# One transformer layer on one core: inverse norms of q and k by eight VectorE steps in place of two GpSimd powers

## The chip, the cores and the metric

The kernel runs on one core of a Trainium2 chip. The metric is the device time of one execution, in microseconds (us); of several executions the median is taken. A core has five engines with a queue each, which run in order and wait for one another by semaphores: TensorE (PE), VectorE (DVE), ScalarE (ACT), GpSimd (POOL) and SyncE (SP, which here only issues DMAs).

## The reference

The input is 32 images of 3x96x96 pixels, cut into 36 patches each: 1152 rows of 768 numbers. The layer is, shortened:

```python
h = layernorm(patches) @ W + b          # 768 -> 192
h = layernorm(h, g2, b2)
x = _layernorm(h); q, k, v = split(x @ in_proj.T + bias)
attn = einsum('nhld,nhmd->nhlm', _normalize(q), _normalize(k))   # 12 heads of 16
attn = softmax(attn * exp(min(logit_scale, ...)))
h = h + (attn @ v * head_scale) @ out_w.T + out_b
y = bitlinear(_layernorm(h), w_in, g_in)         # rms norm, 8-bit rows, ternary weights
up, gate = split(y)
h = h + bitlinear(silu(gate) * up, w_out, g_out)
```

`_normalize` divides each head's 16 numbers of q and of k by their length: a row has 24 inverse square roots of sums of squares. Attention runs over the 32 images at one patch place.

## The kernel before, in words

The 1152 rows are nine tiles of 128 rows, t = 0 to 8, four patch places each. Every tile passes the same stages, and every engine has one list, written out by hand, that interleaves the stages of different tiles. A step is a small function named after what it writes (`ss_(3)` writes `ss` of tile 3), and waits for semaphores that count tiles. Nothing but these lists and waits sets the order.

The stages of a tile, with the engine:

- Embedding: `bst1_`, `mv1_` (DVE: statistics of the pixels), `xp_` (ACT), `xT_` (PE: transposes into banks 0 and 1), `xTe` (ACT), `emb` (PE, bank 7), `ve1_` and `rs1_` (POOL: variance plus epsilon, then power -0.5), `h0s_` (DVE).
- Second norm: `bst2_`, `mv2_`, `hg_`, `h_` (DVE) with `ve2_`, `rs2_` (POOL). Third norm: `bst3_`, `mv3_` (DVE), `ve3_`, `rs3_`, `nm3_` (POOL), `xh_` (ACT).
- q, k, v: `xhT_`, `qkv` (PE), `sq_` (ACT: squares), `qkc`, `vx_` (ACT: copies), `ss_` (DVE: sums of squares, 24 a row), `ssm_` (DVE: these with the logit scale). Then `rnk_` (L317) and `rnq_` (L313), two POOL powers of 12 numbers a row each, and the products `kpad_` (L818) and `qn_` (L809) on DVE, which scale k and q. `kT_` (L828) and `qT_` (L824) are DVE's transposes of them.
- Attention: `sc` (PE, L613: scores), `mx_`, `sm_` (DVE), `pr_` (ACT: exp), `pT_` (DVE, L841), `pv` (PE, L625), `rsum_`, `on_` (DVE), `oT_` (PE, bank 1), `oTe` (ACT), `proj` (PE), `h2_` (DVE, L854).
- First feed-forward product: `bst4_`, `mv4_`, `xc_`, `ax4_` (DVE), `ve4_`, `s4_` (POOL), `an4_`, `ri4_`, `qs4_` (DVE, L878 to L886: the scale of the 8-bit row), `xq_` (ACT), `xqT_` (PE, L648, bank 3), `xqTe` (ACT), `ff1` (PE, L658, banks 2 and 3), `f_h_`, `c5_` (POOL), `th_` (ACT), `yg_`, `yy_` (DVE, L890 and L895: they read banks 2 and 3).
- Second: `yw_` (POOL, L343, 512 wide), `ysq_` (ACT), `ms5_`, `r5_`, `s5_` (POOL), `ax5_`, `an5_`, `ri5_`, `qs5_` (DVE), `yq_` (ACT), `yqT_` (PE), `yqTe` (ACT), `ff2` (PE), `f2_` (POOL), `out_` (DVE, L917), and two DMAs that store the tile.

Weights are prepared in the first third, between the tiles' steps.

Of the kernel before, what the change touches and what calls it, by code (L numbers as in the profile page):

```python
# [42 lines left out]
def vit_layer(nc, x, ln1_g, ln1_b, w_emb, b_emb, ln2_g, ln2_b, w_in_proj, b_in_proj, logit_scale,  # L43
              head_scale, w_out_proj, b_out_proj, w_ff_in, g_in, w_ff_out, g_out, out):
    ctx = ExitStack()
    with ctx:
# [216 lines left out]
        def _(pool):  # L263
# [17 lines left out]
            def ve1_(t):  # L281
                pool.wait_ge(mv1_ok, t + 1)
                nc.gpsimd.tensor_scalar(ve1[:, t, :], mv1[:, t, 1:2], LN_EPS, None, ALU.add).then_inc(ve1_ok, 1)  # L283

# [689 lines left out]
```

## Time and profile before

| what | value |
|---|---|
| median of 3 runs | 154.35 us (154.21 to 155.75) |
| the profiled execution's own time | 155.63 us |
| its span, first to last instruction | 153.8 us |
| PE busy | 109.4 us, 71% |
| VectorE busy | 109.2 us, 71% |
| ScalarE busy | 83.7 us, 54% |
| GpSimd busy | 103.8 us, 68% |
| mean granted TensorE clock | 0.897 of full speed |

The profile is of one execution. A busy time is the part of the span in which an engine works. A group of instructions is shown with its summed time and the mean of one; a wait is the idle time of an engine ahead of an instruction, with what ended it.

### The profile page before, as it was taken

Reading aid. Unit: us, or ns where it says so; the run is one execution under the profiler, and the core shown is the slowest. Engines: PE = TensorE matmul, PEld = TensorE weight load, DVE = VectorE, ACT = ScalarE, POOL = GpSimd, SP = SyncE. Lnnn points to the kernel's source line nnn. Section 1 sums busy time; section 2 is a strip of 40 time slices with the busy share of each in tenths; the row PEclk is TensorE's granted clock in tenths of the full one; section 3 lists DMA queues with packets and bytes.
Section 4 is the critical chain, followed back from the end, with each engine's and each line's share of the span. In section 5 each row is a group of like instructions: output and inputs, shape, how many; then the busy total and the mean of one; then the engine's idle time right before and its main releaser. Section 6 shows DMA issues by size and latency. Waiting matters only on the chain.

```text
span 153.8 us, 4558 instructions
## 1 busy us (share of the span) xinstructions
PE 109.4 (71%) x1784; PEld 84.5 (55%) x1784; DVE 109.2 (71%) x342; ACT 83.7 (54%) x168; POOL 103.8 (68%) x178
## 2 busy tenths in 40 slices
PE   0008997878897889749999879789855966762540
PEld 0008995666786578637878646646634744330320
DVE  3066059849899688846898988976999988747310
ACT  0318435999769273444385667345755366685610
POOL 5006026769599999996589899897988636835500
PEclk9999999999999999975899999758999699689555
DMA  5999999930000000000000000100000000000000
GB/s 105 227 281 185 167 267 203 182 101 2 2 4 0 4 4 0 0 4 4 2 0 4 0 4 4 29 15 11 5 27 4 4 26 15 17 12 27 12 25 26
DMA packets 24092, 7.74 MB, mean 50 GB/s; under 512 B 20038, under 2 KB 23495, under 8 KB 24072
## 3 DMA queue, kind: packets, MB, share of 16 engines
q1 hardware_dynamic: 20310, 6.43, 20.8%
q10 hardware_dynamic: 3762, 1.03, 3.5%
q8 instruction: 14, 0.23, 0.7%
q14 instruction: 6, 0.05, 0.1%
HBM read 6.58 MB, written 0.88 MB: 49 GB/s over the span
## 4 chain that ended last, share of the span: by engine, by line
POOL 34%; PE 28%; DVE 13%; issue 8%; ACT 8%; DMA 4%; ACTq 2%; DVEq 0%; POOLq 0%
POOL rn L317 10%; POOL rn L313 9%; PE bank L658 4%; DMA xs<-in_x_dram 4%; PE bank L583 3%; PE bank L666 3%; DVE bst L751 3%; PE bank L675 3%; PE bank L613 3%; POOL rs L297 3%; PE bank L625 3%; PE bank L518 2%; ACT yq L492 2%; POOL rs L289 2%; ACTq L226 2%
## 5 line engine op out<-in xcount | busy, mean ns | idle before, releaser
L317 POOL TENSOR_TENSOR rn<-ssm,mhalf 128x12 f32<-128x12 f32 x9 | 20.5, 2281 | 2.8 <-DVE ssm L803 2.5
L313 POOL TENSOR_TENSOR rn<-ssm,mhalf 128x12 f32<-128x12 f32 x9 | 21.3, 2372 | 0.4
L583 PE MATMUL bank<-w_emb_g,xT 128*128 128x192 f32 x108 | 20.7, 345 | 1.0 <-DVE h0s L762 1.0
L583 PEld LDWEIGHTS bank<-w_emb_g,xT 128*128 128x128 f32 x108 | 18.7, 202 | 1.5 <-issue 1.5
L574 PE MATMUL bank<-ident,xp 128*128 128x128 f32 x54 | 8.1, 290 | 13.7 <-ACT xp L431 12.2
L343 POOL TENSOR_TENSOR yw<-yy,gout_bc 128x512 f32<-128x512 f32 x9 | 11.4, 1267 | 8.3 <-DVE yy L895 8.2
L574 PEld LDWEIGHTS bank<-ident,xp 128*128 128x128 f32 x54 | 6.7, 149 | 14.1 <-issue 12.9
L751 DVE BATCH_NORM_STATS2 bst<-xs 128x6 f32<-128x384 f32 x18 | 8.7, 540 | 6.6 <-DMA xs<-in_x_dram 6.6
L601 PE MATMUL bank<-w_qkv,xhT 97*128 97x384 f32 (+1 forms) x36 | 12.9, 442 | 0.0
L613 PE MATMUL bank<-kT,qT 32*32 32x64 f32 x432 | 9.5, 240 | 4.0 <-issue 3.7
L602 PE MATMUL bank<-w_qkv,xhT 96*128 96x384 f32 (+1 forms) x36 | 12.4, 425 | 0.0
L431 ACT ACTIVATE xp<-xs,mv 128x768 f32<-128x768 f32 x9 | 8.2, 931 | 6.4 <-DVE mv L755 6.4
L666 PE MATMUL bank<-ident,yq 128*128 128x128 f32 x36 | 7.1, 330 | 6.3 <-ACT yq L492 6.1
L658 PE MATMUL bank<-wi_t,xqT 96*128 96x512 bf16 x36 | 11.2, 441 | 0.2
L613 PEld LDWEIGHTS bank<-kT,qT 32*32 32x32 f32 x432 | 7.8, 120 | 5.5 <-issue 5.5
L625 PE MATMUL bank<-vx,pT 32*32 32x17 f32 x864 | 9.2, 180 | 1.9 <-DVE pT L841 1.0
L488 ACT ACTIVATE ysq<-yy,c 128x512 f32<-128x512 f32 x9 | 6.5, 720 | 7.4 <-DVE yy L895 7.4
L625 PEld LDWEIGHTS bank<-vx,pT 32*32 32x32 f32 x864 | 8.2, 104 | 3.8 <-issue 2.5
L666 PEld LDWEIGHTS bank<-ident,yq 128*128 128x128 f32 x36 | 4.7, 163 | 8.6 <-ACT yq L492 8.5
L283 POOL TENSOR_SCALAR ve<-mv 128x1 f32<-128x1 f32 x9 | 1.9, 219 | 11.0 <-DVE mv L755 10.9
L497 ACT ACTIVATE yqT<-bank,mround 128x512 bf16<-128x512 f32 x9 | 6.2, 685 | 5.0 <-PE bank L666 5.0
L602 PEld LDWEIGHTS bank<-w_qkv,xhT 96*128 96x128 f32 x36 | 7.0, 201 | 2.7 <-issue 0.6
(129 smaller groups left out, 310.8 us busy)
## 6 DMA issues: line engine op xcount, KB each, us to landing
xs<-in_x_dram SPq DMA_DIRECT2D x30, 96.0 KB, 3.6
out_dram<-h_all SPq DMA_DIRECT2D x18, 48.0 KB
wi_raw<-in_L_ffn_w_in_dram SPq DMA_DIRECT2D x1, 768.0 KB, 5.7
xs<-in_x_dram ACTq DMA_DIRECT2D x6, 96.0 KB, 4.1
w_emb_sb<-in_L_tok_W_dram SPq DMA_DIRECT2D x1, 576.0 KB, 7.2
w_qkv_raw<-attn_in_proj_weight_dram ACTq DMA_DIRECT2D x1, 432.0 KB
wo_raw<-in_L_ffn_w_out_dram SPq DMA_DIRECT2D x1, 384.0 KB, 6.6
gout_bc<-in_L_ffn_g_out_dram SPq DMA_DIRECT2D x1, 256.0 KB, 4.8
```

Of the source, the lines that this page charges most:

```text
L313: nc.gpsimd.tensor_tensor(out=rn[:, t, 0:H], in0=ssm[:, t, 0:H], in1=mhalf[:, 0:H], op=ALU.pow).then_inc(rnq_ok, 1)
L317: nc.gpsimd.tensor_tensor(out=rn[:, t, H:2 * H], in0=ssm[:, t, H:2 * H], in1=mhalf[:, 0:H], op=ALU.pow).then_inc(rnk_ok, 1)
L343: nc.gpsimd.tensor_tensor(out=yw[:, s, :], in0=yy[:, s, :], in1=gout_bc[:, :], op=ALU.mult).then_inc(yw_ok, 1)
L574: mm = nc.tensor.transpose(dst, xp[:, t % 3, P * k:P * (k + 1)], ident[:, :])
L583: mm = nc.tensor.matmul(emb_bank, xT[:, t % 3, P * k:P * (k + 1)], w_emb_g[:, 3 * (k % 2) + k // 2, :], start=(k == 0), stop=(k == KF - 1))
L601: nc.tensor.matmul(dst, xhT[:, t % 3, 0, :], w_qkv[:, 0, cols], start=True, stop=False)
L602: mm = nc.tensor.matmul(dst, xhT[0:HC, t % 3, 1, :], w_qkv[0:HC, 1, cols], start=False, stop=True)
L613: mm = nc.tensor.matmul(bank[6][q, 2 * B * a:2 * B * (a + 1)], qT[q, s, B * a:B * (a + 1)], kT[q, s, 2 * B * a:2 * B * (a + 1)], start=Tru ...
L625: mm = nc.tensor.matmul(o_bank[q, h, :], pT[q, s, B * h:B * (h + 1)], vx[q, t, h, :], start=True, stop=True)
L658: mm = nc.tensor.matmul(dst[:, :], xqT[:, t % 3, c, :], wi_t[:, c, FF * half:FF * (half + 1)], start=(c == 0), stop=(c == 1))
L666: mm = nc.tensor.transpose(yqT_bank[:, k, :], yq[:, t % 2, P * k:P * (k + 1)], ident[:, :])
L751: nc.vector.bn_stats(bst1[:, t, n, :], pixels[:, 24 * n:24 * (n + 1), :]).then_inc(bst1_ok, 1)
```

## The change

It has five parts.

1. `rnq_` and `rnk_` are gone. In their place stand eight DVE steps on all 24 numbers of a row: a first guess from the bits of the number taken as an integer (`ry0_`), four steps of a first correction (`ra_`, `rw_`, `rz_`, `ry1_`), three of a second (`rb_`, `rv_`, `rn_`). Constants are folded into `sq_` and `ssm_`.
2. The products `qn_` and `kpad_` move from DVE's list to POOL's.
3. Epsilon enters as a third triple of statistics (count, mean 0, and a constant) that `bn_aggr` adds in, so `ve1_` to `ve4_` are gone and the powers `rs1_`, `rs2_`, `rs3_`, `s4_` read `mv` directly. Eight memsets at the start write the triples.
4. The scale of the 8-bit row: `an4_`, `ri4_`, `qs4_` (three DVE steps) become `m4_`, `qs4_` (two), with a POOL step `e4_` and a factor moved into `gin()`, once.
5. `xqT_` writes bank 1, where `xT_`, `xhT_` and `oT_` write too, not bank 3. All four lists are in a new order.

```diff
-        xqT_bank = bank[3][0:HC, 0:2 * P].rearrange("p (c t) -> p c t", c=2)
+        xqT_bank = small_bank
...
-            def ve1_(t):
                 pool.wait_ge(mv1_ok, t + 1)
-                nc.gpsimd.tensor_scalar(ve1[:, t, :], mv1[:, t, 1:2], LN_EPS, None, ALU.add).then_inc(ve1_ok, 1)
...
-            def rnk_(t):
-                pool.wait_ge(ssm_ok, t + 1)
-                nc.gpsimd.tensor_tensor(out=rn[:, t, H:2 * H], in0=ssm[:, t, H:2 * H], in1=mhalf[:, 0:H], op=ALU.pow).then_inc(rnk_ok, 1)
...
+            def kpad_(t):
+                after(pool, kT_ok, t - 1)
...
+                pool.wait_ge(qk_ok, t + 1)
+                pool.wait_ge(rn_ok, t + 1)
+                nc.gpsimd.tensor_tensor(out=k_slots(t % 2), in0=qk[:, t % 3, D:2 * D].rearrange("p (a b d) -> p a b d", b=2, d=DH),
+                                        in1=rn[:, t, H:2 * H].rearrange("p (a b) -> p a b", b=2).unsqueeze(3)
+                                        .to_broadcast([P, HP, 2, DH]), op=ALU.mult).then_inc(kpad_ok, 1)
...
+            def ry0_(t):
+                dve.wait_ge(ssm_ok, t + 1)
+                nc.vector.tensor_scalar(ry[:, t % 2, 0, :].bitcast(I32), ssm[:, t, :].bitcast(I32), -0.5, RSQRT_MAGIC, ALU.mult,
+                                        ALU.add).then_inc(ry0_ok, 1)
+
+            def ra_(t):
+                dve.wait_ge(ry0_ok, t + 1)
+                nc.vector.tensor_tensor(out=ra[:, t % 2, :], in0=ssm[:, t, :], in1=ry[:, t % 2, 0, :], op=ALU.mult).then_inc(ra_ok, 1)
...
+            def rn_(t):
+                dve.wait_ge(rv_ok, t + 1)
+                nc.vector.scalar_tensor_tensor(out=rn[:, t, :], in0=rv[:, t % 2, :], scalar=-64.0 / 3.0, in1=ry[:, t % 2, 1, :],
+                                               op0=ALU.add, op1=ALU.mult).then_inc(rn_ok, 1)
...
-            def an4_(t):
+            def m4_(t):
                 dve.wait_ge(ax4_ok, t + 1)
-                dve.wait_ge(s4_ok, t + 1)
-                nc.vector.tensor_scalar(an4[:, t, :], ax4[:, t, :], s4[:, t, :], Q_EPS, ALU.mult, ALU.max).then_inc(an4_ok, 1)
...
+                dve.wait_ge(e4_ok, t + 1)
+                nc.vector.tensor_scalar(m4[:, t, :], ax4[:, t, :], e4[:, t, :], 1.0 / QMAX, ALU.max, ALU.mult).then_inc(m4_ok, 1)
```

What the new lists do to an engine's instructions shows at three places. A row is the line, the operation, what it writes and reads, and the shape.

First, VectorE where tiles 3 and 4 are being normalized. Before, the two products of tile 2 and the transposes behind them stand there (kpad and qn wait for POOL's powers):

```order
L818 TENSOR_TENSOR kpad<-qk,rn 128x6x2x16
L832 TENSOR_REDUCE mx<-bank6 128x12
L828 STREAM_TRANSPOSE kT<-kpad 128x384
L836 TENSOR_TENSOR sm<-bank6,mx 128x384
L809 TENSOR_TENSOR qn<-qk,rn 128x192
L841 STREAM_TRANSPOSE pT<-pr 128x384
L824 STREAM_TRANSPOSE qT<-qn 128x192
```

Now, for tile 4, the small steps stand one by one between the instructions of other stages:

```order
L838 SCALAR_TENSOR_TENSOR rz<-rw 128x24
L792 SCALAR_TENSOR_TENSOR hg<-h0s,mv2,g2_bc 128x192
L843 SCALAR_TENSOR_TENSOR ry<-rz,ry 128x24
L886 TENSOR_TENSOR on<-bank5,rsum 128x192
L848 TENSOR_TENSOR rb<-ssm,ry 128x24
L798 SCALAR_TENSOR_TENSOR h_all<-hg,rs2,b2_bc 128x192
L852 TENSOR_TENSOR rv<-rb,ry 128x24
L803 BN_STATS bst3<-h_all 128x6
L856 SCALAR_TENSOR_TENSOR rn<-rv,ry 128x24
```

The products have left this engine, the eight steps have come, and the transposes now wait for POOL's products.

Second, GpSimd around tile 2's powers. Before:

```order
L317 TENSOR_TENSOR rn<-ssm,mhalf 128x12
L313 TENSOR_TENSOR rn<-ssm,mhalf 128x12
L301 TENSOR_SCALAR ve3<-mv3 128x1
L293 TENSOR_SCALAR ve2<-mv2 128x1
L305 TENSOR_TENSOR rs3<-ve3,mhalf 128x1
L297 TENSOR_TENSOR rs2<-ve2,mhalf 128x1
```

Now, around the products of tiles 1 and 2:

```order
L365 TENSOR_TENSOR kpad<-qk,rn 128x6x2x16
L355 TENSOR_TENSOR qn<-qk,rn 128x192
L295 TENSOR_TENSOR rs1<-mv1,mhalf 128x1
L355 TENSOR_TENSOR qn<-qk,rn 128x192
L365 TENSOR_TENSOR kpad<-qk,rn 128x6x2x16
L299 TENSOR_TENSOR rs2<-mv2,mhalf 128x1
```

The wide powers are gone, products stand in their places, and the small powers have no addition ahead of them.

Third, VectorE behind the last tile's `h2_(8)` (the first row of each block; h2_all from bank 7 is `out_`). Before, the next 512-wide step is `ax5_(6)`:

```order
L854 TENSOR_TENSOR h2_all<-bank6,h_all 128x192
L912 TENSOR_SCALAR qs5<-ri5,s5 128x1
L858 BN_STATS bst4<-h2_all 128x6
L862 BN_AGGR mv4<-bst4 128x2
L868 SCALAR_TENSOR_TENSOR xc<-h2_all,mv4,gin_bc 128x192
L873 TENSOR_REDUCE ax4<-xc 128x1
L899 TENSOR_REDUCE ax5<-yw 128x1
```

Now `out_(2)` follows, then `yg_(6)`, `yy_(6)` and `ax5_(5)`:

```order
L891 TENSOR_TENSOR h2_all<-bank6,h_all 128x192
L951 SCALAR_TENSOR_TENSOR h2_all<-bank7,f2,h2_all 128x192
L895 BN_STATS bst4<-h2_all 128x6
L920 RECIPROCAL qs4<-m4 128x1
L942 RECIPROCAL ri5<-an5 128x1
L899 BN_AGGR mv4<-bst4 128x2
L906 SCALAR_TENSOR_TENSOR xc<-h2_all,mv4,gin_bc 128x192
L946 TENSOR_SCALAR qs5<-ri5,s5 128x1
L911 TENSOR_REDUCE ax4<-xc 128x1
L924 SCALAR_TENSOR_TENSOR yg<-th,bank2 128x512
L929 TENSOR_TENSOR yy<-yg,bank3 128x512
L933 TENSOR_REDUCE ax5<-yw 128x1
```

So attention has moved ahead of the feed-forward stages: behind `h2_(8)` stand one `yg_`, one `yy_`, one `ax5_` and three `out_` more than before.

## Rows read from the trace of the kernel before

**Rows 1.** The page: engines with busy us, share of the span, instructions.

```profile
PE 109.4 (71%) x1784; PEld 84.5 (55%) x1784; DVE 109.2 (71%) x342; ACT 83.7 (54%) x168; POOL 103.8 (68%) x178
```

**Rows 2.** The page: the chain that ended last, by engine and by line.

```profile
POOL 34%; PE 28%; DVE 13%; issue 8%; ACT 8%; DMA 4%; ACTq 2%; DVEq 0%; POOLq 0%
POOL rn L317 10%; POOL rn L313 9%; PE bank L658 4%; DMA xs<-in_x_dram 4%; PE bank L583 3%; PE bank L666 3%; DVE bst L751 3%; PE bank L675 3%; PE bank L613 3%; POOL rs L297 3%; PE bank L625 3%; PE bank L518 2%; ACT yq L492 2%; POOL rs L289 2%; ACTq L226 2%
```

**Rows 3.** Busy time by stretch: length, PE, PEld, DVE, ACT, POOL, clock, DMA.

```profile
48.00:64.00 16.00, 13.53 (x344) 11.13 (x335) 13.16 (x44) 7.52 (x18) 15.57 (x22) 1.00 0.01 2
64.00:76.00 12.00, 9.48 (x170) 7.38 (x171) 7.82 (x26) 5.32 (x13) 8.84 (x12) 0.72 0.02 3
76.00:96.00 20.00, 18.40 (x371) 14.14 (x369) 17.71 (x59) 13.62 (x32) 18.16 (x28) 1.00 0.01 2
108.00:124.00 16.00, 11.83 (x400) 8.90 (x400) 15.14 (x43) 9.11 (x19) 12.79 (x21) 0.89 0.04 11
```

**Rows 4.** Groups of GpSimd: the two powers; busy, mean ns, idle before.

```profile
L313 POOL TENSOR_TENSOR rn<-ssm,mhalf 128x12 f32<-128x12 f32 x9 | 21.3, 2372 | 0.4
L317 POOL TENSOR_TENSOR rn<-ssm,mhalf 128x12 f32<-128x12 f32 x9 | 20.5, 2281 | 2.8 <-DVE ssm L803 2.5
```

**Rows 5.** Timeline: start, us, engine, instruction, wait; waits on GpSimd, and a power.

```profile
39.49 0.38 DVE L809 TENSOR_TENSOR qn<-qk,rn 128x192 f32<-128x192 f32 x1 [0.15 <-POOL rn L313]
...
51.81 2.27 POOL L313 TENSOR_TENSOR rn<-ssm,mhalf 128x12 f32<-128x12 f32 x1
...
51.95 0.36 DVE L818 TENSOR_TENSOR kpad<-qk,rn 128x192 f32<-128x192 f32 x1 [1.39 <-POOL rn L317]
...
95.64 0.36 DVE L809 TENSOR_TENSOR qn<-qk,rn 128x192 f32<-128x192 f32 x1 [0.72 <-POOL rn L313]
...
96.99 0.99 PE L625 MATMUL bank<-vx,pT 32*32 32x17 f32 x96 [1.03 <-DVE pT L841]
...
102.49 0.38 DVE L818 TENSOR_TENSOR kpad<-qk,rn 128x192 f32<-128x192 f32 x1 [0.59 <-POOL rn L317]
```

**Rows 6.** Timeline of VectorE: how soon the next instruction starts.

```profile
52.23 0.55 DVE L832 TENSOR_REDUCE mx<-bank 128x12 f32<-128x384 f32 x1
...
56.38 0.17 DVE L803 SCALAR_TENSOR_TENSOR ssm<-ss,ls_div 128x24 f32<-128x24 f32 x1
56.48 0.35 DVE L788 BATCH_NORM_STATS2 bst<-h_all 128x6 f32<-128x192 f32 x1
...
63.38 0.12 DVE L882 RECIPROCAL ri<-an 128x1 f32<-128x1 f32 x1
63.53 0.21 DVE L886 TENSOR_SCALAR qs<-ri,s 128x1 f32<-128x1 f32 x1
```

**Rows 7.** Timeline: GpSimd and VectorE instructions that overlap.

```profile
86.48 1.02 DVE L777 SCALAR_TENSOR_TENSOR hg<-h0s,mv,g_bc 128x192 f32<-128x192 f32 x1
...
110.23 1.26 POOL L343 TENSOR_TENSOR yw<-yy,gout_bc 128x512 f32<-128x512 f32 x1
...
110.36 1.35 DVE L818 TENSOR_TENSOR kpad<-qk,rn 128x192 f32<-128x192 f32 x1
...
131.42 0.59 DVE L868 SCALAR_TENSOR_TENSOR xc<-h_all,mv,gin_bc 128x192 f32<-128x192 f32 x1
```

**Rows 8.** Timeline of the end: the last h2, tiles 7 and 8, the last out.

```profile
130.43 0.34 DVE L854 TENSOR_TENSOR h_all<-bank,h_all 128x192 f32<-128x192 f32 x1
...
136.51 0.69 DVE L895 TENSOR_TENSOR yy<-yg,bank 128x512 f32<-128x512 f32 x1
...
137.34 0.40 PE L648 MATMUL bank<-ident,xq 128*96 128x128 f32 x2 [0.42 <-DVE yy L895]
...
138.30 1.04 PE L658 MATMUL bank<-wi_t,xqT 96*128 96x512 bf16 x4
...
140.83 0.68 DVE L895 TENSOR_TENSOR yy<-yg,bank 128x512 f32<-128x512 f32 x1
...
148.61 0.42 DVE L917 SCALAR_TENSOR_TENSOR h_all<-bank,f,h_all 128x192 f32<-128x192 f32 x1 [2.32 <-PE bank L675]
```

More of the change, by code:

```diff
@@ L934, in _ @@
-            hg_(8); ax5_(1); h2_(3); ss_(6); h_(8); bst4_(3); ssm_(6); rsum_(4); an5_(1); mv4_(3); on_(4); xc_(3); bst3_(8)
-            ax4_(3); mv3_(8); ri5_(1); qs5_(1); yg_(2); mx_(5); kpad_(6); yy_(2); kT_(6); sm_(5); qn_(6); out_(0); an4_(3)
-            pT_(5); ss_(7); h2_(4); qT_(6); bst4_(4); ssm_(7); rsum_(5); mv4_(4); ax5_(2); xc_(4); on_(5); ax4_(4); mx_(6)
-            out_(1); sm_(6); ri4_(3); qs4_(3); kpad_(7); pT_(6); kT_(7); an4_(4); an5_(2); ri4_(4); ri5_(2); qs4_(4)
-            qs5_(2); ss_(8); h2_(5); ssm_(8); bst4_(5); mv4_(5); xc_(5); qn_(7); ax4_(5); yg_(3); qT_(7); yy_(3); rsum_(6)
@@ L939, in _ @@
-            out_(2); kpad_(8); on_(6); kT_(8); mx_(7); ax5_(3); sm_(7); an5_(3); ri5_(3); qs5_(3); an4_(5); yg_(4); pT_(7)
-            yy_(4); h2_(6); ri4_(5); qn_(8); bst4_(6); qs4_(5); qT_(8); mv4_(6); rsum_(7); xc_(6); on_(7); ax4_(6); ax5_(4)
-            mx_(8); an5_(4); sm_(8); an4_(6); ri5_(4); out_(3); qs5_(4); pT_(8); ri4_(6); qs4_(6); yg_(5); h2_(7); yy_(5)
-            bst4_(7); rsum_(8); mv4_(7); on_(8); xc_(7); ax4_(7); ax5_(5); out_(4); an4_(7); ri4_(7); qs4_(7); yg_(6)
-            an5_(5); yy_(6); ri5_(5); h2_(8); qs5_(5); bst4_(8); mv4_(8); xc_(8); ax4_(8); ax5_(6); an4_(8); an5_(6)
@@ new lines, in _ @@
+            qT_(4); xc_(0); h_(8); ax4_(0); m4_(0); qs4_(0); bst3_(8); mx_(4); ss_(5); sm_(4); ssm_(5); rsum_(2); on_(2)
+            pT_(4); h2_(1); ry0_(5); bst4_(1); mv4_(1); ra_(5); rw_(5); xc_(1); rz_(5); ax4_(1); ry1_(5); rb_(5); mv3_(8)
+            m4_(1); rv_(5); rn_(5); ss_(6); qs4_(1); ssm_(6); yg_(0); ry0_(6); kT_(5); rsum_(3); qT_(5); yy_(0); h2_(2)
+            on_(3); bst4_(2); ra_(6); mv4_(2); xc_(2); rw_(6); ax4_(2); rz_(6); ax5_(0); mx_(5); m4_(2); ry1_(6); qs4_(2)
+            sm_(5); yg_(1); rb_(6); yy_(1); ss_(7); ssm_(7); h2_(3); rv_(6); ry0_(7); bst4_(3); ra_(7); rsum_(4); mv4_(3)
@@ new lines, in _ @@
+            rn_(6); an5_(0); pT_(5); rw_(7); ax5_(1); rz_(7); xc_(3); ry1_(7); on_(4); qT_(6); ri5_(0); rb_(7); yg_(2)
+            an5_(1); kT_(6); rv_(7); yy_(2); ax4_(3); m4_(3); ri5_(1); rn_(7); qs4_(3); ss_(8); mx_(6); ssm_(8); ax5_(2)
+            sm_(6); kT_(7); ry0_(8); rsum_(5); ra_(8); pT_(6); rw_(8); h2_(4); rz_(8); qT_(7); ry1_(8); on_(5); rb_(8)
+            bst4_(4); rv_(8); qs5_(0); mv4_(4); yg_(3); rn_(8); qs5_(1); yy_(3); mx_(7); xc_(4); sm_(7); rsum_(6); ax4_(4)
+            on_(6); pT_(7); h2_(5); m4_(4); kT_(8); qs4_(4); qT_(8); an5_(2); bst4_(5); rsum_(7); mv4_(5); ax5_(3); xc_(5)
@@ L949 @@
+            qs5_(7); ax5_(8); out_(5); an5_(8); ri5_(8); qs5_(8); out_(6); out_(7); out_(8)
 _INS = ['x', 'L0_tok_ln1_g', 'L0_tok_ln1_b', 'L0_tok_W', 'L0_tok_b', 'L0_tok_ln2_g', 'L0_tok_ln2_b',
```

286 lines of the change are left out of this document (152 added, 134 removed).

## The prediction

> **What bounds the kernel now.** I read the page's engine line first: PE, VectorE and GpSimd are each busy about 70% of the span, ScalarE 54% [rows 1]. So no engine is the bound by its total. The chain that ended last says who holds the others up: GpSimd has 34% of it, and the two powers of `rnk_` and `rnq_` alone 20%, some 30 us of 153.8 [rows 2]. They are 18 instructions of about 2.3 us, 41.8 us of GpSimd's 103.8 [rows 4]. Next the stretches. From 48 to 64 us GpSimd is busy 15.6 of 16 us and VectorE 13.2: here GpSimd is the bound. But from 76 to 96 PE has 18.4 of 20, GpSimd 18.2 and VectorE 17.7, and from 108 to 124 VectorE has 15.1 of 16 [rows 3]. The reader is to see that behind GpSimd two engines stand close: what is taken off GpSimd can be won only as far as PE and VectorE have idle time, and this change puts work on VectorE. So I count the idle of VectorE that GpSimd causes, then what VectorE gets in addition.
>
> The first 35 us (loading, embedding, weights) and the store at the end I take as unchanged: the new PE list embeds four tiles ahead of the first q, k and v and the old one three, but by then the same work is done.
>
> **Part 1, the waits on GpSimd.** Between 35 and 124 us VectorE waits 13 times for a GpSimd result: the first is 0.15 us at 39.49, the longest 1.39 at 51.95, the last 0.59 at 102.49 [rows 5]. They sum to 6.5 us. With 41.8 us less of powers, and the four additions of epsilon gone too, GpSimd has slack, and I let them all go: **-6.5**. In place of the wait for a power, `kT_` and `qT_` wait for a product; the new list puts at least three instructions between `rn_` and the transposes, so I price that at nothing; if that cover is gone it costs up to a product's length in each of nine tiles. What VectorE no longer delays is late next at PE: at 96.99 PE waits 1.03 us for `pT`, which stood behind a `qn` that waited for a power [rows 5]. **-1.0**. VectorE's other waits in this part are for PE and ScalarE; below nothing and above 5 us can come of them, and I take 0.
>
> **Part 2, VectorE's own work.** What does a small step cost in a full queue? `ssm` has the same 24 numbers: it takes 0.17 us, but the next instruction starts 0.10 us after it [rows 6]. 72 steps at 0.10 are 7.2 us. In nine places two steps that depend on each other are adjacent and the second must wait for the first to end: some 0.12 more each, 1.1. Together **+8.3**. The bounds are 0.10 and 0.22 a step (its length and a hand-over), so 7 to 16. The page "VectorE: DVE Perf Modes" of the Trainium skill, section "The DRAIN you can't avoid", says that the next instruction does not start until the pipe of the one before is empty. By that rule a step costs its whole 0.17, 5 us more in all; the row with 0.10 speaks against it for instructions that don't depend on each other. The result is rival D.
>
> The 18 products leave VectorE: from the start of `kpad` at 51.95 to the next start at 52.23 are 0.28 us [rows 5, 6], and 18 of 0.27 are **-4.9**. The scale of the 8-bit row loses one step of three, `ri` to `qs` is 0.15 [rows 6], nine times: **-1.3**. `bn_aggr` reads three numbers more: nothing.
>
> **Part 3, who holds whom.** In this trace VectorE instructions with two inputs in SBUF don't run while GpSimd streams `yw`. The `kpad` that starts at 110.36, inside the `yw` of 110.23 to 111.49, takes 1.35 us where others take 0.36, and ends 0.2 us behind `yw`. There are five such cases among nine `yw`: the first is `hg` at 86.48 with 1.02 us, the last `xc` at 131.42 with 0.59 [rows 7]; together they cost 2.9 us. Two of them, 1.9 us, were `kpad` and `qn`, which leave: **-1.9**. A power doesn't hold VectorE: the `kpad` at 51.95 runs its 0.36 us inside a power that began at 51.81 [rows 5].
>
> The change replaces 18 instructions that hold nobody by 18 that stream 192 columns with two inputs, and gives VectorE 11 two-input instructions a tile for 6: about one per us. A product's length on GpSimd isn't in this trace. From below it is the 0.36 us of VectorE's own, from above `yw`'s 1.26 for 512 columns. It is nearest to `yw`, the same operation: by columns 0.47, with a fixed part of 0.2, 0.6 us. A hold of L us that meets such an instruction after 1 us on average costs L - (1 - e^-L): 0.15 us for 0.6, so 18 products cost 2.7. For `yw` I walk the new list: behind `yy_(0)` to `yy_(3)` a two-input step comes within a us, behind the later ones not; about 2.6 us in place of the 1.0 that is left. Together **+4.4**, between 0 and 13.
>
> The page "SBUF — State Buffer" of the Trainium skill, section "Terms", says that GpSimd and VectorE share a pair of ports, that it is held for a whole instruction, and that the loser is blocked entirely. By that rule the powers would have held VectorE too, and the change would win much more; the `kpad` inside a power says no, the `kpad` inside `yw` yes. The sum goes by the rows.
>
> **Part 4, the end.** The new lists put attention ahead. Behind `h2_(8)` VectorE has one `yg_`, one `yy_`, one `ax5_` and three `out_` more than before. Priced by `yy` (0.69) and `out` (0.42) [rows 8] that is 3.3 us which no longer stand ahead of `h2_(8)`: **-3.3**. Does the tail grow by it? Before, it took from 130.43 to 149.03, 18.6 us. From `yy_(7)` at 136.51 to `yy_(8)` at 140.83 are 4.3 us, and in them `xqT` waits for `yy` because it writes bank 3 and `ff1` starts 0.96 us behind it. In bank 1 it no longer waits: 3.4 us a tile. After `h2_(8)`, `xqT_(6)`, its copy and `ff1` take about 2.5 us, `th`, `yg`, `yy` 2.3, two more tiles 6.7, and from the last `yy`'s end at 141.5 the rest is 7.5 as before: 19.0 us. **+0.4**. This end is a chain of latencies with VectorE mostly idle, so the added work hides in it.
>
> **The sum.** -6.5 - 1.0 + 8.3 - 4.9 - 1.3 - 1.9 + 4.4 - 3.3 + 0.4 = -5.8 us. The profiled execution, 155.6 us with 153.8 of span, would be 149.8; the median of the three runs lies 1.3 us lower, and from 154.35 the sum gives **148.5 us**. VectorE would be busy about 114 us, GpSimd about 70.
>
> **The rivals.**
>
> A, more is won. PE's clock is granted at 0.72 of full speed in two stretches, 64 to 76 [rows 3] and 96 to 108: over half of each at 1.2 GHz in place of 2.4, after a time in which PE had little to do. If a better fed PE keeps the higher level in one of them, up to 3.4 us of PE's time go. Against it: not all of PE's gaps have to do with GpSimd. 145 us.
>
> B, the other side: the products on GpSimd are slow. They read one input with a broadcast and write `kpad` in pieces of 16, of which the trace shows nothing. At 1.26 us each the holds cost 18 x 0.54 = 9.8 in place of 2.7, 155.6 us: that is where it decides. At 1.45 us they cost 13, and the time is 159. The page "GPSIMD Engine Reference" of the Trainium skill, section "When to use GPSIMD", advises against just this: elementwise work with two inputs on GpSimd at about half VectorE's speed. That alone would be harmless here, with GpSimd idle half the time.
>
> C, bank 1 becomes a queue: `xT_`, `xhT_`, `oT_` and `xqT_` of a tile must each wait for ScalarE's copy of the one before. `xqT`'s end to `ff1`'s start, the time of such a copy, is 0.56 us [rows 8]. Nine more copies on PE's path cost up to 5.0: 153.5 us. For it: PE has 92% between 76 and 96, with no room to lose it. Against it: the list puts another matmul group between most such pairs.
>
> D, each step costs its whole length of 0.17 us or a little over, because nearly each depends on the last but one. +5 us, 153.5.
>
> That the change doesn't do what it says is not one: it isn't left to a compiler.
>
> **How the numbers follow.** The forecast 0.50, A 0.16, B 0.08, C 0.14, D 0.12. The forecast's own range is 146.5 to 151. About 1% is what a measurement can tell from no change: under 152.8 is faster, over 155.9 slower. The forecast and A are faster, and of C and D together (0.26) 0.06 where half the loss comes true, 0.19 within 1% and 0.01 above; B is slower. Faster 0.72, within 1% 0.19, slower 0.09. The range reaches from 143, A with both stretches in part, to 155.5, C and D with some of each, and leaves B out.
>
> **What would show it.** Right: no VectorE wait on a power; `kpad` and `qn` on GpSimd near 0.6 us; a VectorE busy time of 112 to 117 us; starts 0.10 apart behind a step; `h2_(8)` some 6 us earlier than 130.4 and 19 us from there to the last `out_`; VectorE over 90% busy from 48 to 110. Wrong: products of 1 us or more with VectorE instructions of over a us beside them (B); PE waits ahead of `xqT` and `xhT` for ScalarE (C); steps 0.2 apart (D); an end that begins at 130 as before.

## The result, and the profile after

The changed kernel takes 140.08 us (median of 4 runs, 138.75 to 140.78) against 155.05 us (154.21 to 156.39) on the same chip: 0.902 of the time before, with a 95% interval of 0.891 to 0.913. That is faster, by 15 us where 6 were forecast, and it lies below the range of 143 to 155.5. (Medians and ranges in this document are of all runs of a kernel; a ratio and its interval compare only the runs within 1.5% of the kernel's fastest.)

The page of the changed kernel: its span, the engines with busy us, share and instructions, and the slices of VectorE, GpSimd and of the granted clock (one digit is a fortieth of the span):

```profile
span 138.7 us, 4589 instructions
PE 105.4 (76%) x1784; PEld 82.0 (59%) x1784; DVE 108.2 (78%) x388; ACT 81.6 (59%) x168; POOL 66.0 (48%) x160
DVE  4059028999999999999999998959999999695210
POOL 7003001565329621486136866614874798787000
PEclk9999999999999999999999997579999997797555
PE 30%; DVE 30%; ACT 13%; POOL 9%; issue 8%; DMA 4%; ACTq 2%; DVEq 0%
```

The last of these lines is the chain that ended last. GpSimd had 34% of it and has 9% [rows 2]; it is busy 66.0 us in place of 103.8. VectorE is busy as long as before, 108.2 us against 109.2 [rows 1], in a span 15 us shorter. From the seventh slice to the 34th it is hardly idle but in one.

Where the 15 us went is read from the stretches. The borders are 35 us (to there I had assumed no change), the start of `h2_(8)` and the end of the last `out_`. Before, then after (length, then busy us with the number of instructions of PE, PEld, DVE, ACT, POOL, then the clock, the DMA share and GB/s):

```profile
0.00:35.00 35.00, 19.92 (x119) 18.22 (x120) 18.36 (x61) 17.42 (x33) 13.88 (x44) 1.00 0.99 189
35.00:130.40 95.40, 79.23 (x1622) 60.80 (x1620) 81.01 (x253) 55.66 (x117) 80.93 (x116) 0.91 0.03 7
130.40:149.05 18.65, 10.20 (x44) 5.44 (x44) 9.87 (x31) 10.65 (x19) 9.00 (x19) 0.73 0.06 18
```

```profile
0.00:35.00 35.00, 22.19 (x134) 20.38 (x135) 20.16 (x65) 18.10 (x34) 10.23 (x39) 1.00 1.04 189
35.00:113.30 78.30, 70.89 (x1593) 54.38 (x1592) 75.06 (x287) 49.87 (x110) 43.36 (x95) 0.96 0.02 5
113.30:132.90 19.60, 12.29 (x60) 7.24 (x58) 12.95 (x40) 13.65 (x26) 12.36 (x27) 0.74 0.09 28
```

Length less VectorE's busy time is its idle time, and everything up to the last `out_` is one or the other:

| VectorE, us | before | after | change | forecast |
|---|---|---|---|---|
| idle, first 35 us | 16.6 | 14.8 | -1.8 | 0 |
| idle, 35 us to `h2_(8)` | 14.4 | 3.2 | -11.2 | -7.5 |
| idle, from there to the last `out_` | 8.8 | 6.7 | -2.1 | -2.9 |
| busy, all three | 109.2 | 108.2 | -1.1 | +4.6 |
| sum | 149.05 | 132.9 | -16.2 | -5.8 |

The storing behind the last `out_` became 1.1 us longer, so the span is 15.1 us shorter. (The forecast's idle of the last stretch is the tail's +0.4 less the 3.3 us of work that moved into it.) The miss of about 10 us has two halves: VectorE's own work, which did not grow (5.7 us), and idle time that I had not counted (4.7).

The waits say which idle time of the middle went. In the kernel before, the longest groups of VectorE's waits there are these (engine, line, what it waits for, us in total, times, longest):

```profile
DVE kpad L818 <- POOL rn L317: 3.1, 4, 1.4
DVE mx L832 <- PE bank L613: 2.4, 2, 2.1
DVE yg L890 <- ACT th L483: 2.1, 3, 1.2
DVE qn L809 <- POOL rn L313: 1.7, 4, 0.7
DVE ss L796 <- ACT sq L450: 1.5, 2, 1.3
DVE h_all L783 <- POOL rs L297: 1.1, 3, 0.6
```

The middle of the changed kernel has only these:

```profile
DVE ss L811 <- ACT sq L460: 1.1, 1, 1.1
DVE rsum L882 <- PE bank L636: 0.7, 1, 0.7
DVE mx L869 <- PE bank L624: 0.4, 1, 0.4
```

By engine waited for, with the small groups: GpSimd 6.5 us before and none after, PE 3.1 and 1.1, ScalarE 3.6 and 1.1.

### The profile page after: what moved, and what is told of

It reads as the page before. It is cut to its first block, busy times and chain, and to the rows that moved or that the text cites. A ratio compares the mean times of both kernels' runs of the same rounds, so it can differ in the third digit from the quotient of the medians.

```text
span 138.7 us, 4589 instructions
## 1 busy us (share of the span) xinstructions
PE 105.4 (76%) x1784; PEld 82.0 (59%) x1784; DVE 108.2 (78%) x388; ACT 81.6 (59%) x168; POOL 66.0 (48%) x160
## 4 chain that ended last, share of the span: by engine, by line
PE 30%; DVE 30%; ACT 13%; POOL 9%; issue 8%; DMA 4%; ACTq 2%; DVEq 0%
PE bank L612 5%; PE bank L594 4%; PE bank L613 4%; DMA xs<-in_x_dram 4%; PE bank L624 4%; POOL yw L337 3%; PE bank L585 3%; PE bank L529 2%; DVE pT L878 2%; DVE bst L764 2%; DVE mx L869 2%; ACTq L232 2%; PE bank L686 2%; ACT xp L441 2%; DVE ax L933 1%
## 5 line engine op out<-in xcount | busy, mean ns | idle before, releaser
L594 PE MATMUL bank<-w_emb_g,xT 128*128 128x192 f32 x108 | 19.6, 331 | 0.0
L594 PEld LDWEIGHTS bank<-w_emb_g,xT 128*128 128x128 f32 x108 | 17.4, 190 | 0.6 <-ACT xT L448 0.2
L299 POOL TENSOR_TENSOR rs<-mv,mhalf 128x1 f32<-128x1 f32 x9 | 5.3, 589 | 19.6 <-DVE mv L786 19.6
L669 PE MATMUL bank<-wi_t,xqT 96*128 96x512 bf16 x36 | 10.2, 409 | 1.4 <-ACT xqT L488 1.2
L612 PEld LDWEIGHTS bank<-w_qkv,xhT 97*128 97x128 f32 x36 | 6.6, 204 | 5.7 <-issue 2.6
L447 ACT ACTIVATE xT<-bank 128x512 f32<-128x512 f32 x9 | 5.3, 591 | 7.7 <-PE bank L585 7.6
L295 POOL TENSOR_TENSOR rs<-mv,mhalf 128x1 f32<-128x1 f32 x9 | 5.2, 582 | 8.4 <-DVE mv L770 8.4
L624 PE MATMUL bank<-kT,qT 32*32 32x64 f32 x432 | 8.6, 227 | 0.5 <-DVE h_all L891 0.5
L474 ACT ACTIVATE pr<-sm 128x384 f32<-128x384 f32 x9 | 4.7, 523 | 6.9 <-DVE sm L873 6.9
L624 PEld LDWEIGHTS bank<-kT,qT 32*32 32x32 f32 x432 | 7.1, 112 | 2.5 <-issue 2.5
L460 ACT ACTIVATE sq<-bank 128x384 f32<-128x384 f32 x9 | 4.3, 482 | 7.1 <-PE bank L613 7.1
```

The source lines that it names most:

```text
L299: nc.gpsimd.tensor_tensor(out=rs2[:, t, :], in0=mv2[:, t, 1:2], in1=mhalf[:, 0:1], op=ALU.pow).then_inc(rs2_ok, 1)
L594: mm = nc.tensor.matmul(emb_bank, xT[:, t % 3, P * k:P * (k + 1)], w_emb_g[:, 3 * (k % 2) + k // 2, :], start=(k == 0), stop=(k == KF - 1))
L612: nc.tensor.matmul(dst, xhT[:, t % 3, 0, :], w_qkv[:, 0, cols], start=True, stop=False)
L624: mm = nc.tensor.matmul(bank[6][q, 2 * B * a:2 * B * (a + 1)], qT[q, s, B * a:B * (a + 1)], kT[q, s, 2 * B * a:2 * B * (a + 1)], start=Tru ...
L669: mm = nc.tensor.matmul(dst[:, :], xqT[:, t % 3, c, :], wi_t[:, c, FF * half:FF * (half + 1)], start=(c == 0), stop=(c == 1))
```

## The experiments

A kernel is compared with the kernel before on the same chip, whose medians in the later calls were 154.9 to 157.4 us. In words: "old" and "new order" are the four lists, "the new parts" are parts 1 to 4 of the change and bank 1.

### One part alone in the old order

**The powers' time alone.** The operation of `rnq_` and `rnk_` is a product, in the same places and with the same waits; the inverse norms are left out of the computation.

```diff
-in1=mhalf[:, 0:H], op=ALU.pow).then_inc(rnk_ok, 1)
+in1=mhalf[:, 0:H], op=ALU.mult).then_inc(rnk_ok, 1)
```

> The kernel before with its old order, in which GpSimd multiplies by a constant where it took the 18 wide powers (the inverse norms are left out, so q and k are scaled wrongly). No new work on VectorE. Theory P (the powers held up the whole pipeline, and whatever order stands around them, their removal gives most of the gain of 15 us): 141 to 144 us. Theory O (the old lists were laid out around the powers, and only the new order turns the free time into a gain): 147 us or more, as much as VectorE's own waits on GpSimd, 6.5 us and 1 of PE's, allow.

Measured: 154.77 us (152.03 to 157.06), ratio 0.987 (0.945 to 1.030). GpSimd falls from 103.8 to 65.6 us of work and little comes of it (the theory of the order, 147 us or more, fits; that of the powers, 141 to 144, does not). Waits of VectorE from 35 us to `h2_(8)`:

```profile
DVE mx L832 <- PE bank L613: 3.1, 3, 2.1
DVE yg L890 <- ACT th L483: 2.3, 2, 1.2
DVE rsum L845 <- PE bank L625: 2.2, 2, 2.0
DVE ss L796 <- ACT sq L450: 2.0, 2, 1.8
DVE pT L841 <- ACT pr L464: 1.3, 3, 0.6
```

None names GpSimd any more: I was right that all those waits [rows 5] go. But they are replaced. The stretch's VectorE idle is 13.8 us here (94.24 less 80.45 busy), 14.4 before. `h2_(8)` starts at 129.24, 1.2 us earlier. With two smaller groups VectorE's waits for PE and ScalarE sum to 12.3 us, where they were 6.7. The order was laid for an engine that was late; each VectorE instruction now comes at once to the next thing that isn't ready. One thing besides differs: in this trace PE's mean clock is 0.859, not 0.897, and its busy time 112.3 us, not 109.4, so a part of the new waits for PE can come from there.

**The eight steps alone, and with the products on GpSimd.** The steps stand between VectorE's other instructions; in the second kernel `kpad_` and `qn_` stand in GpSimd's list where the powers stood.

```diff
-rnk_(2); rnq_(2); ve3_(4)
+ve3_(4)                     # steps, products on VectorE
+kpad_(2); qn_(2); ve3_(4)   # steps, products on GpSimd
```

> The kernel before with its old order; the powers are replaced by the eight VectorE steps, one behind each of the next instructions after ssm, and the two products stay on VectorE. Theory P: the gain of the run without powers less the price of 72 steps, 5 to 8 us, so 147 to 151. Theory O: 152 us or more, since the old order wins at most 7.5 us and the steps cost 8.3.

> As the run before it, but with the two products on GpSimd, at the places where the two powers stood: the whole new arithmetic of the norms in the old order. Theory P: 4 us less than with the products on VectorE (18 of 0.27 us, less what they hold), 143 to 147. Theory O: no gain by the products, since the old order has kT and qT close behind the places of the products: 150 us or more.

Measured: 159.0 us (156.31 to 162.02), ratio 1.015 (0.971 to 1.059), and 158.09 us (151.09 to 161.06; there is no interval for it). VectorE is busy 114.5 us in the first. These kernels scatter by 6 and 10 us, more than any part is worth, so neither can be placed against the kernel before (153.95 to 159.59 in that call), nor can the theories be told apart. What can be said is that no run of either comes near 140; the lowest of the eight is 151.09 us, of the second kernel.

### The new order with one part undone

**The old norms in the new order.** `rnk_` and `rnq_` stand where the products stood on GpSimd, and the products are back on VectorE; everything else is new.

```diff
-rs2_(4); kpad_(0); nm3_(3); rs2_(5); qn_(0)
+rs2_(4); rnk_(0); nm3_(3); rs2_(5); rnq_(0)
```

> The changed kernel with its new order, epsilon triple and bank 1, but with the old arithmetic of the norms: two powers of 12 on GpSimd a tile, at the places of the products, and the products on VectorE just ahead of the transposes. Theory P: the powers cost their 41.8 us of GpSimd again and the time goes back to 152 or more. Theory O: the new order alone is worth half of the gain or more, 145 to 148.

Measured: 163.09 us (162.99 to 163.54), ratio 1.052 (1.039 to 1.066). The expected half of the gain from the order alone did not come. The new order is 5% slower than the old one with the norms it was not made for. The waits, in the same form:

```profile
DVE kpad L825 <- POOL rn L315: 8.7, 7, 1.8
DVE qn L816 <- POOL rn L311: 5.5, 5, 1.7
DVE mx L839 <- PE bank L614: 3.8, 4, 2.1
PE bank L614 <- DVE qT L831: 4.2, 2, 3.3
```

VectorE waits 14.2 us for powers, where all its waits on GpSimd before were 6.5, and PE up to 3.3 us for a transpose that stands behind them.

**The changed kernel again; twice the steps; no steps.** The first is no edit. The second adds a dummy step on 24 numbers behind each of the eight (72 more). The third leaves the steps out and with them the inverse norms; `rn_` is one `min`.

```diff
+rn_(0); dum_(7, 0); ssm_(1)    # twice
-ry0_(1); ra_(1); rw_(1); rz_(1); ry1_(1); rb_(1); rv_(1); rn_(1)
+rn_(1)                         # none
```

> The changed kernel once more, so that the three runs with it stand against it on one chip. 139 to 141 us if its time does not depend on the chip as that of the kernel before seems to (154 to 160 in the first four runs).

> The changed kernel with a ninth to sixteenth step a tile: behind each of the eight VectorE steps a multiplication of the same 24 numbers into a spare buffer that nobody reads. 72 instructions more on VectorE. Theory V (between 35 us and the last h2 VectorE is the bound of the changed kernel, 96% busy, so what is added to it is added to the time): 0.10 us each, 147 us, or 145 if a step costs 0.07. Theory L (the time is set by the latencies between engines, VectorE's queue has slack): under 142 us.

> The changed kernel with one VectorE instruction a tile in place of the eight steps (a minimum with a constant; the inverse norms are left out). 63 instructions less on VectorE. Theory V: up to 6 us less, 134 to 136 us, less if PE, 91% busy in that part, becomes the bound. Theory L: 139 to 140.

Measured: 141.2 us (138.47 to 142.46) beside 156.2 for the kernel before; 144.48 us (144.06 to 146.78), ratio 0.928 (0.920 to 0.936); 139.54 us (138.27 to 141.25), ratio 0.890 (0.880 to 0.899). Their pages:

```profile
PE 108.8 (77%) x1784; PEld 84.2 (60%) x1784; DVE 108.7 (77%) x388; ACT 81.5 (58%) x168; POOL 66.0 (47%) x160
...
PE 108.5 (78%) x1784; PEld 84.0 (60%) x1784; DVE 102.2 (73%) x325; ACT 81.7 (59%) x168; POOL 66.2 (47%) x160
```

(The changed kernel again, and the one without steps.) 72 steps more are 5.2 to 5.7 us of VectorE, 0.07 to 0.08 each, and 3.3 us of time. 63 fewer are 6.0 to 6.5 us, about 0.10 each, and 1.7 us of time. So a step costs VectorE what `ssm` showed [rows 6]. What it costs in time is less sure: by the ratios to the kernel before, 72 more are 4 us and 63 fewer 2 us, and the intervals of the changed kernel (0.891 to 0.913) and of the one without steps overlap. Work added to VectorE so lengthens the time by more than half of itself, and work taken away gives back a third or less; the first result lies between the two theories (144.48, for 145 to 147 or under 142), the second at that of the latencies (139 to 140). Without steps PE is busy 78% of the span and VectorE 73%, which suggests that PE bounds next.

**The products on VectorE,** just ahead of their transposes.

```diff
-nc.gpsimd.tensor_tensor(out=qn[:, t % 3, :]
+nc.vector.tensor_tensor(out=qn[:, t % 3, :]
```

> The changed kernel with the two products back on VectorE, just ahead of their transposes; GpSimd has neither powers nor products. Theory V: 18 of 0.27 us are 4.9 more for VectorE, less the 1.7 us that GpSimd's products and yw hold it now: 142 to 145 us. Theory L: the way to GpSimd and back falls out, 138 to 140.

Measured: 143.74 us (143.46 to 145.6), ratio 0.927 (0.918 to 0.936), 2.5 us over the median of the changed kernel of that call and 4 us by the ratios, as expected with VectorE as the bound (142 to 145). VectorE is at 113.5 us: 4.8 to 5.3 us for 18, 0.27 to 0.29 each.

**The additions of epsilon back on GpSimd** (`ve1_` to `ve4_`, adding nothing, ahead of each power).

```diff
-rs1_(0); rs1_(1); rs2_(0)
+ve1_(0); rs1_(0); ve1_(1); rs1_(1); ve2_(0); rs2_(0)
```

> The changed kernel with the four small GpSimd additions a tile put back ahead of the powers rs1, rs2, rs3 and s4 (they add zero, since the triple already carries epsilon). 36 instructions of 0.2 us on GpSimd, 8.9 us of its time. Theory V (VectorE and PE bound the changed kernel, GpSimd has slack): within 1 us of the changed kernel's 140. Theory L (latencies between engines set the time): 36 hand-overs of 0.25 us, 5 us more where a quarter or more of them is on the path, 142 to 146.

Measured: 142.5 us (141.72 to 145.22), ratio 0.920 (0.914 to 0.926), against 0.902 (0.891 to 0.913). So the triple is worth 2 to 3 us. I had counted it at nothing, because GpSimd would have slack. It has, but an addition also stands on each tile's path from the statistics to the norm: in this trace VectorE waits 3.1 us for the results behind such additions (`rs` 1.9, `e` 1.2), and the changed kernel's has no such wait of 0.2 us or more.

**`xqT_` in bank 3**, with its wait for `yy_`, in the new order.

```diff
-xqT_(1, (xhT_ok, 8))
+xqT_(1, (xhT_ok, 8), (yy_ok, 1))
```

> The changed kernel with the transposes of the 8-bit rows in bank 3 again, so that they wait for yy of the tile before. By the forecast's working this costs 0.9 us for each tile at the end where the feed-forward loop is the only work, three tiles, so 142 to 143. If the share of bank 1 costs PE as much as it saves: 139 to 141.

Measured: 147.33 us (145.16 to 147.45), ratio 0.947 (0.936 to 0.957), 7 us more, where 2 to 3 were expected. PE's waits for `yy` in the kernel before, one of them in the rows of the end [rows 8], and in this trace:

```profile
PE bank L648 <- DVE yy L895: 0.8, 2, 0.4
PE bank L659 <- DVE yy L929: 6.5, 5, 1.7
```

Three of the five stand ahead of `h2_(8)`, which starts 3.6 us later than in the changed kernel (116.92 us), and two behind it; the end is 2.8 us longer.

### The other corners

**The scores behind a cover, and bank 1, in the old order.** PE pauses for some 2 us inside rows of small matmuls with nothing to wait for. In the kernel before, and at two places in the one without powers:

```profile
64.80 0.99 PE L625 MATMUL bank<-vx,pT 32*32 32x17 f32 x96
65.66 0.65 PE L613 MATMUL bank<-kT,qT 32*32 32x64 f32 x32
68.38 0.65 PE L613 MATMUL bank<-kT,qT 32*32 32x64 f32 x16 [2.08 <-issue]
```

```profile
65.33 0.65 PE L613 MATMUL bank<-kT,qT 32*32 32x64 f32 x16 [1.98 <-issue]
...
95.53 0.28 PE L625 MATMUL bank<-vx,pT 32*32 32x17 f32 x6 [2.02 <-issue]
```

Both have `sc_(3)` directly behind `pv_(2)`, 144 small matmuls in a row. The edit puts another matmul group between such pairs, at three places ("apart" in what follows); "bank 1" moves `xqT_` there, with the waits that this needs. "Without powers" leaves the inverse norms out, as above.

```diff
-pv(2, (vx_ok, 5)); sc(3, (h2_ok, 2)); xhT_(5, (xT_ok, 16)); ff1(0); oT_(2, (xhT_ok, 6))
+pv(2, (vx_ok, 5)); xhT_(5, (xT_ok, 16)); ff1(0); sc(3, (h2_ok, 2)); oT_(2, (xhT_ok, 6))
...
-xqT_bank = bank[3][0:HC, 0:2 * P].rearrange("p (c t) -> p c t", c=2)
+xqT_bank = small_bank
```

> The kernel before, with three groups of PE moved in its list so that the scores (48 small matmuls) no longer stand directly behind the 96 small matmuls of pv: the scores of tiles 2 and 3 behind the next group or the one after, pv of tile 7 ahead of the projection. Theory G (PE's pauses of about 2 us marked issue, and the low clock after them, come from these runs of small matmuls, and are a part of what the new order saves): 2 to 5 us less than the kernel before, 150 to 153. If the pauses are bound to a place in the program or hidden: no change, 154 to 158.

> The same three moves in the kernel before with its powers replaced by multiplications (inverse norms left out), which took 154.8 us. Theory G: 149 to 152, since without the powers PE is what VectorE waits for. If the pauses don't matter: 154 to 156.

> The kernel before with the transposes of the 8-bit rows in bank 1 and ff1 waiting for yy in their place; nothing else. Theory S (each part is worth little alone, because in the old lists another engine's wait takes the place of the one removed): within 2 us of the kernel before, 153 to 157. Theory A (the parts add up): 7 us less, as much as going back to bank 3 cost the changed kernel, 147 to 149.

> The old order without powers (inverse norms left out) and with the scores apart from pv, which took 151.4 us, and bank 1 in addition. Theory S: 149 to 152. Theory A: 144 to 146.

Measured: the kernel before with the scores apart takes 155.2 us (154.13 to 156.89), ratio 1.003 (0.999 to 1.007): the pause, which is gone from its trace, cost it nothing, likely because GpSimd was late anyway. Without powers it is 151.42 us (150.78 to 153.74), ratio 0.979 (0.974 to 0.983), where the same kernel with the pauses had 0.987 (0.945 to 1.030): by the medians 3 us, by the intervals open. (Only the pause in the scores went; the one in `pv` is still there, 1.75 us.) Without powers, with these three moves, the old order does gain 2%. Bank 1 in the kernel before gave 161.37, 163.78 and 157.35 us and one run of 347, so it has no interval; two of the three lie above every run of the kernel before in that call (153.98 to 161.31). Without powers and apart, bank 1 gives 159.72 us (158.64 to 160.82), ratio 1.034 (1.025 to 1.043), 8 us over the same kernel with bank 3. The bank that gains 7 us in the new order costs 8 in the old one; neither theory had it, for either kernel. In the trace of the second PE waits 3 us more for ScalarE's copies of `xT` and `xqT`, and its mean clock is 0.836, where it was 0.883; how the 8 us divide isn't shown.

**All new parts in the old order.** Steps, products, triples, scale and bank 1 are new; the lists are the old ones, with the new names where the old ones stood. The second kernel has the scores apart as well.

```diff
-rnk_(2); rnq_(2); ve3_(4); ve2_(5); rs3_(4); rs2_(5)
+kpad_(2); qn_(2); rs3_(4); rs2_(5)
...
-pv(2, (vx_ok, 5)); sc(3, (h2_ok, 2)); xhT_(5, (xT_ok, 16))
+pv(2, (vx_ok, 5)); sc(3, (h2_ok, 2)); xhT_(5, (xT_ok, 16), (xqT_ok, 1))
```

> Every part of the change (steps, products on GpSimd, epsilon as a triple, two steps for the scale, bank 1) in the old order of all four lists: the steps one behind each of the instructions that follow ssm, the products where the powers stood. The output is the reference's. Theory S: 150 us or more, so that the order is worth 10 us or more. Theory A: 143 to 146, the order being worth 3 to 6 (my forecast gave it 3).

> The same with the scores moved apart from pv as in e11 and e12. Theory S with PE as the next bound (as e12 showed 3.4 us less without powers): 2 to 4 us less than e15. If PE's pauses are not what holds this kernel: the same as e15.

Measured: 163.14 us (160.77 to 165.3), ratio 1.044 (1.034 to 1.055). Apart, 159.46 us (153.94 to 165.42), ratio 0.998 (0.990 to 1.006), which rests on 3 of its 10 runs: the three moves are worth 4 us by the medians and 7 by the ratios. The 2 us pause in `pv` is in both traces. The stretch from 35 us to `h2_(8)`, and rows of the waits, of the first:

```profile
35.00:134.63 99.63, 84.31 (x1625) 64.63 (x1623) 80.04 (x303) 56.20 (x118) 47.33 (x103) 0.84 0.03 7
...
POOL kpad L365 <- DVE rn L857: 37.2, 9, 5.9
...
DVE yg L925 <- ACT th L493: 4.4, 3, 1.7
DVE rsum L883 <- PE bank L636: 3.9, 3, 2.3
DVE mx L870 <- PE bank L624: 2.3, 2, 1.9
DVE pT L879 <- ACT pr L474: 2.0, 4, 0.6
```

and one of PE, its `xqT_` behind ScalarE's copy out of the shared bank:

```profile
64.54 0.40 PE L659 MATMUL bank<-ident,xq 128*96 128x128 f32 x2 [1.89 <-ACT xT L448]
```

VectorE has 80.0 us of work there and 19.6 of idle, against 75.1 and 3.2 in the new order. GpSimd waits 37 us at `kpad`: it is no longer the late one, and nobody gains by it. PE and ScalarE are (150 us or more was the expectation if a removed wait only moves), and PE's clock is granted at 0.84, not 0.96. The four corners:

| | old norms and products | new parts |
|---|---|---|
| old order | 155.1 us | 163.1 us, 1.044 |
| new order | 163.1 us, 1.052 | 140.1 us, 0.902 |

(Lower left has the new triples, scale and bank.) As these lists stand, neither the parts nor the order is worth anything alone; the two together are worth 15 us. Given the new parts, the order is worth 23 us against the old lists as they stood, and 15 by the ratio of the kernel with the scores apart. Bank 1 likely has a large share in the 163.1 of the upper right corner: it cost 8 us in the old order without powers.

One thing goes along with the corners and was never held still: the clock. For the same 1784 matmuls PE is busy 116.4 and 116.5 us in the two bad corners (mean clock 0.835 and 0.844), 109.4 us before (0.897) and 105.4 in the changed kernel (0.918). The kernel before alone, in one call, took 154.07 us with a mean clock of 0.904 and 161.31 with 0.832. In the traces the clock falls in or behind long gaps of PE (at 67 us before, at 85 us after), so it is likely in part a result of the order. How much of the 15 and of the 23 us comes by way of the clock, and how much by things being ready in time, no run here shows.

**Not tried:** one engine's new list with the old lists of the others. They wait for one another in a circle, so which moves of the new order matter most stays open.

## Why the prediction was right or wrong

**Part 1, "I let them all go: -6.5" and "I take 0"** for VectorE's waits for PE and ScalarE. This is the step that failed. The waits on GpSimd went, as said (6.5 us to none). But in the old order they came back as waits for PE and ScalarE (idle 14.4 to 13.8 us, first experiment). I argued from the old trace as if the instructions behind each wait were ready. With the new lists the waits for PE and ScalarE fall too, from 6.7 to 2.2 us, where I took no change: the middle's idle fell by 11.2 us, 3.7 over the forecast. My bound for these waits, "below nothing and above 5 us", held, and I took its wrong end. That the -6.5 itself fits is luck, for its reason does not: without the powers and with the old order the idle fell by 0.6 us. The removal of the powers makes the room, and the order uses it. I read the order only for what it adds behind `h2_(8)`.

**"In place of the wait for a power, `kT_` and `qT_` wait for a product", priced at nothing.** Right: no VectorE wait on GpSimd is among the rows of the middle.

**"The first 35 us ... I take as unchanged".** Wrong by 1.8 us. VectorE does 20.2 us of work there, not 18.4, and PE 22.2, not 19.9. The new lists begin more work early; I had looked only at how many tiles are embedded.

**Part 2, steps "+8.3", products "-4.9", scale "-1.3".** The steps at 0.10 each came out as 6.8 to 7.4 us for 72 (kernel without steps), so rival D, a step at its whole length, is out: `ssm`, `rn` and the like take 0.17 and cost 0.10. The page "VectorE: DVE Perf Modes" of the Trainium skill, section "The DRAIN you can't avoid", says that the next instruction does not start until the pipe is empty; with 0.17 a step that is an estimate of 12 us, and the runs side with the row. The products were worth 4.8 to 5.3; the scale was not run by itself. That is about 1 us of the 5.7 us by which VectorE's work was over-forecast.

**Part 3, holds: "-1.9", "+4.4".** Over-sized, and the second half of the miss: net -0.2 in place of +2.5. A product takes 0.51 us on GpSimd, not 0.6. By line, engine and operation, with the busy us, the mean ns and the idle time ahead:

```profile
L365 POOL TENSOR_TENSOR kpad<-qk,rn 128x192 f32<-128x192 f32 x9 | 4.8, 531 | 6.1 <-DVE rn L856 6.1
L355 POOL TENSOR_TENSOR qn<-qk,rn 128x192 f32<-128x192 f32 x9 | 4.6, 511 | 3.2 <-DVE rn L856 3.1
```

VectorE instructions held by GpSimd, each inside the row above it:

```profile
80.93 1.26 POOL L337 TENSOR_TENSOR yw<-yy,gout_bc 128x512 f32<-128x512 f32 x1 [0.65 <-DVE yy L929]
...
81.35 0.89 DVE L818 SCALAR_TENSOR_TENSOR ssm<-ss,ls_div 128x24 f32<-128x24 f32 x1
...
85.24 0.51 POOL L365 TENSOR_TENSOR kpad<-qk,rn 128x192 f32<-128x192 f32 x1
85.30 0.48 DVE L838 SCALAR_TENSOR_TENSOR rz<-rw 128x24 f32<-128x24 f32 x1
...
88.87 1.26 POOL L337 TENSOR_TENSOR yw<-yy,gout_bc 128x512 f32<-128x512 f32 x1 [0.87 <-DVE yy L929]
89.28 0.89 DVE L856 SCALAR_TENSOR_TENSOR rn<-rv,ry 128x24 f32<-128x24 f32 x1
```

`ssm` and `rn` take 0.17 us elsewhere; here each ends 0.05 us behind the end of its `yw`. The mechanism is right: seven small steps are longer than 0.2 us, and all seven lie inside such a stream of GpSimd. Together they lose 2.7 us, 2.0 to `yw` and 0.7 to products. I had forecast 2.7 for products: I let each meet a two-input instruction at random, while the list puts transposes, reductions and statistics beside most of them. The 2.9 us of holds before [rows 7] thus became 2.7. These terms account for about 4 of the 5.7 us; the rest of 1 to 2 I can't assign. So VectorE's busy time, 108.2 us, lies below the 112 to 117 that I had named as a sign of being right.

**Part 4 and the tail, "-3.3" and "+0.4", 19.0 us.** Right for the tail, 19.6 us, with VectorE's work there up from 9.9 to 13.0. (`h2_(8)` itself starts 17.1 us earlier, where some 6 were forecast.) The forecast cycle of 3.4 us a tile is what is there:

```profile
120.43 0.69 DVE L929 TENSOR_TENSOR yy<-yg,bank 128x512 f32<-128x512 f32 x1
...
123.83 0.69 DVE L929 TENSOR_TENSOR yy<-yg,bank 128x512 f32<-128x512 f32 x1
...
132.45 0.42 DVE L951 SCALAR_TENSOR_TENSOR h_all<-bank,f,h_all 128x192 f32<-128x192 f32 x1 [2.04 <-PE bank L686]
```

But I weighed bank 1 as a gain at this one place, 0.9 us a tile, and in the middle only as a cost (rival C). In the new order it is worth 7 us. The end's share of it is 2.8 us, three tiles of 0.9 as I had priced it; the 3.6 us ahead of `h2_(8)`, where PE waits for `yy` in three more tiles, I had left out.

**Epsilon's additions "gone too", at no gain:** 2 to 3 us, as measured.

**The rivals.** B, slow products, is out: 0.51 to 0.53 us each, and taking them back to VectorE costs 2.5 us or more. (Its working has a slip: by the formula for holds, products of 1.45 us cost 12.3 us, not 13.) The advice of the page "GPSIMD Engine Reference" of the Trainium skill, section "When to use GPSIMD", is borne out in the speed (0.51 against 0.27 to 0.29 us a product) and not in the result, since GpSimd was idle half of the time. C is out for the new order; in the old one bank 1 did cost 8 us. A's condition came true, and for both of its stretches: from 64 to 76 us [rows 3] and from 96 to 108 the clock was 0.72 and is 1.00. Its mean rose from 0.897 to 0.918, and PE's busy time fell by 4.0 us. What that is worth in time no run separates from the order. One low stretch is left in the middle, from 85 to 92 us. It begins behind two gaps of PE, a pause and a wait:

```profile
83.36 0.30 PE L636 MATMUL bank<-vx,pT 32*32 32x17 f32 x13 [1.65 <-issue]
...
86.62 1.62 PE L612 MATMUL bank<-w_qkv,xhT 97*128 97x384 f32 x2 [1.76 <-DVE on L886]
```

**The chances.** Right in sign. The case that I gave 0.50, with its own range of 146.5 to 151, did not come. The whole range was too narrow below because every case in it let VectorE's waits for PE and ScalarE stand; none said that a new order might remove that as well.

## What to carry to other kernels

Where engines run lists laid out by hand, taking a cost away mostly moves the wait to whoever is next, so price a change together with its order: for each long wait of the engine that will be the bound, whoever causes it, ask whether the new lists still have it. To test it, run the four corners, part and order each old and new: one part at a time in the old order would have said here that hardly anything is worth having. Read the granted clock of each corner as well, since it can move along with the order. And walk every place at which a shared bank is waited for, not just the clearest one.

## What was not expected of the hardware

PE stops for 1.2 to 2.3 us inside long rows of small matmuls, with no semaphore to wait for. In the changed kernel it stops ahead of the last 13 matmuls of one `pv`, for 1.65 us, and at the same matmul when it ran again (1.38 us) and without steps (1.38). With dummy steps, or with the products on VectorE, PE's list is the same and no pause is longer than 0.6 us, so the list of PE alone does not fix it. A packet of the queue that loads instructions begins 0.5 to 1 us ahead of each of the five pauses that I looked at; others, as one between 70 and 72 us before, have no pause behind them. That the one causes the other is not shown. In the kernel before the pause in the scores costs nothing; with all new parts in the old order the three moves that remove the one in the scores give 2 to 5%. The clock was granted at the lower of PE's two levels, 1.2 GHz, from 68 to 74 us before, where it falls within the pause that ends at 68.38, and from 85 to 92 us after, behind the pause that ends at 83.36 and a second gap of 1.8 us.

A VectorE instruction that reads two inputs in SBUF and starts beside a `yw` or a product of GpSimd is held to its end, however short it is: `ssm`, 0.17 us elsewhere, takes 0.89 beside `yw`. One that takes one of its two inputs from a bank is not: `h2_` at 108.99 us keeps its 0.34 us inside the `yw` of 108.78 to 110.05. The smaller the work, the larger the share: the 24-number steps added here are as easily caught as a 192-wide product was.
